# Pair-mask sums, test and subtraction on GpSimd in a graph network's first row stage

## Chip, cores and metric

The kernel runs on one core of one Trainium2 chip. The metric is device time in microseconds; the time given is the median of three runs.

## What is computed

The reference takes 1250 nodes of 512 features and 20,000 edges (`src`, `dst`). Four layers follow each other, each added to the rows: a message-passing layer over the edges, a layer of 64 routed experts, a graph network of four blocks, and a gated feed-forward layer with ternary weights. The change touches what the third layer needs from the edges. Its attention is sparse:

```
scores = einsum('ehd,ehd->eh', q[src], k[dst])
smax   = segment_max(scores, src);  ex = exp(scores - smax[src])
denom  = segment_sum(ex, src);      attn = ex / denom[src]
out    = segment_sum(attn[:, :, None] * v[dst], src)
```

The kernel computes it densely, over all 1250 x 1250 pairs of nodes. An edge that occurs c times counts c times, which is a term log(c) on the score; a pair without an edge must vanish, which is a very large term of the other sign. That term, for all pairs, is the mask. A node with no outgoing edge has an output of zero, for which a flag for each row (`linked`) is kept. All four blocks read the same mask.

## The kernel before

The rows are ten tiles of 125. While the earlier layers run, each edge is counted into one of two count tables in HBM (`pairs`, 1250 x 1250 float32 each). The first row stage (`rows_stage` with source "first" and sink "qkv") then does two things side by side.

**Its main work.** For each row tile VectorE and ScalarE make normalised and modulated rows, TensorE turns them, and ScalarE and VectorE write them as a high part and a low part (`y_high`, `y_low`; in a product of two such numbers three of the four part products are taken). VectorE's shift instruction is at L1873. Then TensorE works through 24 units (L1437), each three part products over four 128-row blocks: units 0 to 11 give q, units 12 to 23 give k, each in three spans of 500, 374 and 376 rows, with two PSUM banks in turn, so unit n waits until unit n-2 has been taken. ScalarE takes q units alone (`qT`, L1771); of k units ScalarE takes `k_high` (L1777) and VectorE then `k_low` (L1900). Before unit 12 wk must be split into high and low parts (`set_a_high` by ScalarE, `set_a_low` by VectorE, L1856, four pieces, placed after n = 7 in both engines' orders); before the v tiles wv is split likewise (`set_b`, placed after n = 21, behind the masks' work of that n). Wq's low parts come from GpSimd (L1624), which does nothing else here. The ten v tiles (L1446) end the stage: VectorE adds the bias (L1962), ScalarE copies the high part and VectorE subtracts the low one (L1973).

**The mask.** For tile t the two counts are loaded into `pair_c[t]` and `pair_m[t]`. VectorE adds them in place and keeps the row maximum in `pair_top` (L1908), ScalarE takes Ln(count + 1e-18) in place (L1784) and writes Relu(-1e28 log - 1e28) to `pair_m[t]` (L1786), which is zero where a pair has an edge, and VectorE subtracts the logarithm (L1914). SP stores the result in `mask_d`. Where this work stands in each engine's order is written by hand: after unit n of its loop, VectorE does the sums with COUNT_AT[t] = n and then the subtractions with CAP_AT[t] = n, ScalarE the logarithms with LOG_AT[t] = n. Each engine runs its instructions strictly in that order.

**Buffers and SP's order.** Twelve buffers serve ten tiles in pairs, so tiles 6 to 9 reuse buffers of tiles whose masks are stored. SP issues every load and store, in this order: loads of tiles 0 to 5, a store of the rows, stores of masks 0 to 3, load 6 (once mask 0 is stored), store 4, load 7 (once mask 1 is stored), the next conditioning weights `cw`, the v bias and wv, a wait until `cw` has landed, store 5, load 8 (once mask 2 is stored), load 9 (once masks 3 and 5 are stored), then stores 6 to 9. ScalarE's k_high of unit 12 waits until three masks are made, its copies of v tiles 0, 2, 4 and 7 until seven, eight, nine and ten are. The attention that follows (L2041, L2144, L2185) reads the masks from HBM; L2185 is GpSimd's scaling of the probabilities with 1/denominator and `linked`.

The semaphores `counted`, `logd`, `capped` and `mask_made` count the tiles through the four steps.

Of the kernel before, what the change touches and what calls it, by code (L numbers as in the profile page):

```python
# [17 lines left out]
ACT = mybir.ActivationFunctionType  # L18
ALU = mybir.AluOpType
# [3 lines left out]
P = 125  # L23
NT = N // P
# [1431 lines left out]
class Map:  # L1456
# [4 lines left out]
    def __init__(self, nc, base):  # L1461
# [32 lines left out]
        self.tiny, self.far = at("tiny", 153536, [128, 1]), at("far", 153568, [128, 1])  # L1494
# [4 lines left out]
COUNT_AT = (3, 4, 5, 6, 8, 9, 12, 13, 15, 17)  # L1499
LOG_AT = (4, 5, 6, 7, 9, 10, 13, 14, 16, 18)  # L1500
CAP_AT = (5, 6, 8, 9, 10, 11, 14, 16, 18, 19)
TINY, BIG = 1.0e-18, 1.0e28


def rows_stage(nc, T, M, source, sink, g_d, x_d, loads, late, bias, bqk, bvo, last=False, pairs=None, mask_d=None):
# [11 lines left out]
             "pair_in0 pair_in1 pair_in2 pair_in3 pair_in4 pair_in5 pair_in6 pair_in7 pair_in8 pair_in9 counted consts logd capped mask_made "  # L1517
             "mask_out0 mask_out1 mask_out2 mask_out3 mask_out4 mask_out5 mask_out6 mask_out7 mask_out8 mask_out9")
    with Stage(nc, names) as (cw_ready, cw_next, b_in, a_in, w_in, v_in, a_high, a_cut, b_high, b_cut, v_high, v_cut,
# [5 lines left out]
                              counted, consts, logd, capped, mask_made, mask_out0, mask_out1, mask_out2, mask_out3, mask_out4,  # L1525
# [19 lines left out]
        with nc.Block() as block:  # L1545
# [59 lines left out]
            def _(pool):  # L1605
# [36 lines left out]
                if masks:  # L1642
                    nc.gpsimd.memset(M.tiny[:], TINY).then_inc(consts, 1)
                    nc.gpsimd.memset(M.far[:], -BIG).then_inc(consts, 1)
# [81 lines left out]
            def _(act):  # L1726
# [53 lines left out]
                def logarithm(t):  # L1780
                    if t == 0:
                        act.wait_ge(consts, 2)
                    act.wait_ge(counted, t + 1)
                    s.activation(M.pair_c[t][:], M.pair_c[t][:], ACT.Ln, bias=M.tiny[0:P, :]).then_inc(logd, 1)  # L1784
                    act.wait_ge(logd, t + 1)
                    s.activation(M.pair_m[t][:], M.pair_c[t][:], ACT.Relu, bias=M.far[0:P, :], scale=-BIG).then_inc(capped, 1)  # L1786
# [62 lines left out]
            def _(dve):  # L1849
# [53 lines left out]
                def masking(n):  # L1903
                    for t in range(NT) if masks else ():
                        if n == COUNT_AT[t]:
                            c = M.pair_c[t][:]
                            dve.wait_ge(pair_in[t], 64)
                            v.tensor_tensor_reduce(c, c, M.pair_m[t][:], 1.0, 0.0, ALU.add, ALU.max,  # L1908
                                                   M.pair_top[:, t:t + 1]).then_inc(counted, 1)
                    for t in range(NT) if masks else ():  # L1910
                        if n == CAP_AT[t]:
                            c = M.pair_c[t][:]
# [747 lines left out]
```

## Time and profile before

| | before |
|---|---|
| median of 3 runs | 2878.57 us (2877.28 to 2882.2) |
| profiled execution | 2881.81 us, span of its trace 2880.0 us |
| mean granted TensorE clock | 0.945 of full |
| first row stage | 943 to 1096 us of the span |

A span is the time from the first to the last instruction of one profiled execution. Busy time of an engine leaves out its waits; a wait is the idle time just before an instruction, put down to what released it. PE is TensorE, PEld its weight loads, DVE is VectorE, ACT ScalarE, POOL GpSimd, SP SyncE, and `ps` is PSUM. A granted clock of 1.00 is TensorE at 2.4 GHz, 0.50 at 1.2 GHz.

### The profile page before, as it was taken

Reading aid. Unit: us, or ns where it says so; the run is one execution under the profiler, and the core shown is the slowest. Engines: PE = TensorE matmul, PEld = TensorE weight load, DVE = VectorE, ACT = ScalarE, POOL = GpSimd, SP = SyncE. Lnnn points to the kernel's source line nnn. Section 1 sums busy time; section 2 is a strip of 40 time slices with the busy share of each in tenths; the row PEclk is TensorE's granted clock in tenths of the full one; section 3 lists DMA queues with packets and bytes.
Section 4 is the critical chain, followed back from the end, with each engine's and each line's share of the span. In section 5 each row is a group of like instructions: output and inputs, shape, how many; then the busy total and the mean of one; then the engine's idle time right before and its main releaser. Section 6 shows DMA issues by size and latency. Waiting matters only on the chain. (4 is left out here: it accounts for less than half of the span.)

```text
span 2880.0 us, 38762 instructions
## 1 busy us (share of the span) xinstructions
PE 2520.4 (88%) x13585; PEld 2166.2 (75%) x13585; DVE 1861.9 (65%) x3526; ACT 1396.8 (49%) x2764; POOL 1139.5 (40%) x850
## 2 busy tenths in 40 slices
PE   3999999746766668999999999989999989998999
PEld 3788878546556557887877877978978878877997
DVE  2899999564651745767646777457776367667862
ACT  1566566422245635655436655346654356544431
POOL 2788888853673002226003243013260022363420
PEclk9999999867878789999999999999999999999999
DMA  7444344238535752102221011111022030121101
GB/s 253 89 86 86 74 91 83 20 92 268 128 91 175 196 157 62 45 1 72 68 61 46 18 55 53 52 53 36 18 71 68 20 89 19 45 82 34 56 13 35
DMA packets 172076, 220.33 MB, mean 77 GB/s; under 512 B 111791, under 2 KB 120426, under 8 KB 164465
## 3 DMA queue, kind: packets, MB, share of 16 engines
q1 hardware_dynamic: 85134, 189.35, 22.6%
q0 software_dynamic: 86752, 28.51, 5.8%
q8 instruction: 111, 1.82, 0.3%
q14 instruction: 79, 0.65, 0.1%
HBM read 177.10 MB, written 40.15 MB: 75 GB/s over the span
## 5 line engine op out<-in xcount | busy, mean ns | idle before, releaser
L2185 POOL TENSOR_SCALAR prob<-prob,rden,linked 125x1250 f32<-125x1250 f32 x160 | 223.5, 1397 | 955.6 <-DVE rden L2152 955.6
L579 POOL DMA_INDIRECT pairs<-late_cnt,late_idx x160 | 351.1, 2195 | 125.5 <-DMA pairs<-late_cnt,late_idx 75.7
L2103 ACT CAST prob_high<-ps 125x375 fp32r<-125x375 f32 (+1 forms) x480 | 231.1, 503 | 267.1 <-PE ps L2065 261.8
L2144 DVE CUSTOM_DVE_ANT_0 prob<-ps,mask 125x1250 f32<-125x1250 f32 x160 | 233.0, 1456 | 130.1 <-PE ps L2041 109.1
L2157 DVE TENSOR_TENSOR prob_low<-ps,prob_high 125x375 fp32r<-125x375 f32 (+1 forms) x480 | 269.6, 585 | 46.6 <-ACT prob_high L2103 46.6
L338 POOL DMA_INDIRECT Hg<-h_rows,dsti x160 | 230.1, 1438 | 117.3 <-issue 94.0
L2054 PE MATMUL ps<-ident,prob 125*125 125x125 f32 x1600 | 252.3, 273 | 17.3 <-POOL prob L2185 10.7
L2054 PEld LDWEIGHTS ps<-ident,prob 125*125 125x125 f32 x1600 | 232.3, 187 | 29.7 <-POOL prob L2185 22.9
L538 PE MATMUL ps<-onehot,mhi 125*128 125x512 f32 (+1 forms) x960 | 245.7, 364 | 6.1 <-DVE onehot L426 5.9
L538 PE MATMUL ps<-onehot,mlo 125*128 125x512 f32 (+1 forms) x960 | 238.8, 357 | 0.0
L2095 ACT ACTIVATE prob<-prob,top 125x1250 f32<-125x1250 f32 x160 | 214.7, 1342 | 46.3 <-DVE top L2144 37.6
L2065 PE MATMUL ps<-prob_high,v_high 125*128 125x376 f32 (+1 forms) x480 | 211.1, 440 | 4.6 <-ACT qT L2107 3.0
L2041 PE MATMUL ps<-k_high,q_high 128*125 128x512 f32 (+1 forms) x480 | 173.9, 362 | 28.5 <-DVE q_low L2133 19.0
L538 PEld LDWEIGHTS ps<-onehot,mhi 125*128 125x128 f32 x960 | 158.4, 191 | 42.6 <-issue 13.4
L538 PEld LDWEIGHTS ps<-onehot,mlo 125*128 125x128 f32 x960 | 157.5, 191 | 28.2
L2041 PE MATMUL ps<-k_low,q_high 128*125 128x512 f32 (+1 forms) x480 | 172.5, 359 | 0.0
L2041 PE MATMUL ps<-k_high,q_low 128*125 128x512 f32 (+1 forms) x480 | 171.6, 358 | 0.0
L2065 PE MATMUL ps<-prob_low,v_high 125*128 125x376 f32 (+1 forms) x480 | 169.0, 352 | 0.0
L2065 PE MATMUL ps<-prob_high,v_low 125*128 125x376 f32 (+1 forms) x480 | 169.0, 352 | 0.0
L426 DVE TENSOR_SCALAR onehot<-iota_n,srcf 125x1250 fp32r<-125x1250 int16 x120 | 121.0, 1030 | 24.3 <-PEq L71 12.1
L2041 PEld LDWEIGHTS ps<-k_high,q_high 128*125 128x125 f32 x480 | 90.9, 189 | 50.3 <-DVE q_low L2133 20.7
L2330 POOL TENSOR_SCALAR neg<-raw,qsc 128x128 bf16<-128x128 f32 x132 | 78.6, 614 | 119.3 <-DVEq L2352 119.3
(442 smaller groups left out, 5952.4 us busy)
## 6 DMA issues: line engine op xcount, KB each, us to landing
mask<-mask_d SPq DMA_DIRECT2D x40, 546.9 KB
sg_wd<-L_ffn_Wd SPq DMA_DIRECT2D x32, 512.0 KB, 7.2
w_ring<-L_ffn_Wd SPq DMA_DIRECT2D x16, 1024.0 KB, 14.8
w_ring<-L_ffn_Wu SPq DMA_DIRECT2D x16, 1024.0 KB, 5.8
pairs<-zeros POOLq DMA_DIRECT2D x18, 625.0 KB, 25.2
keyrow<-keys_d SPq DMA_DIRECT2D x40, 244.1 KB
kept<-g_d SPq DMA_DIRECT2D x40, 224.0 KB
g_d<-kept SPq DMA_DIRECT2D x30, 224.0 KB
```

The lines of the kernel that those rows point to most:

```text
L338: nc.gpsimd.indirect_dma_start(Hg[:, g % 2, j, :, :].rearrange("p c f -> p (c f)"), None, h_rows[:, :], bass.IndirectOffsetOnAxis(dsti[:, ...
L426: v.tensor_scalar(onehot[:, j, :], T.iota_n[0:P, :], srcf[:, column(g, j):column(g, j) + 1], None, ALU.is_equal).then_inc(hot_ready, 1)
L538: ins = nc.tensor.matmul(agg_chunk(T, a, c), part[:, u, j, a * 128:(a + 1) * 128], onehot[:, j, n0:n0 + nn], start=first and k == 0 and c < 2,
L579: nc.gpsimd.indirect_dma_start(pairs[a][:, :], bass.IndirectOffsetOnAxis(T.E.late_idx[:, c:c + 1], 0), T.E.late_cnt[:, c:c + 1], None, com ...
L2041: ins = nc.tensor.matmul(S(u)[0:P, n0:n0 + nn], M.qr[x][:, b % 2, i * P:(i + 1) * P], M.k[y][:, h, n0:n0 + nn], start=n == 0, stop=n == 2)
L2054: ins = nc.tensor.transpose(T.ps[0:P, 3 + s % 4, i * P:(i + 1) * P], M.prob[:, (FIRST[b] + i) % RING, j * P:(j + 1) * P], T.ident[0:P, 0:P])
L2065: ins = nc.tensor.matmul(T.ps[:, 7, 0:w], M.v[x][:, j, h * DH:(h + 1) * DH], M.pt[y][:, s % 3, 0:w], start=j == 0 and n == 0, stop=j == NT ...
L2095: s.activation(M.prob[:, u % RING, :], M.prob[:, u % RING, :], ACT.Exp, bias=M.top[:, u % RING:u % RING + 1], scale=-1.0, accum_out=M.den[ ...
L2103: s.copy(M.pt[0][:, n % 3, 0:w], T.ps[0:P, 3 + n % 4, 0:w]).then_inc(high, 1)
L2144: v.tensor_tensor_reduce(M.prob[:, r, :], S(u)[0:P, 0:N], M.mask[:, it % MASKS, :], 1.0, 3.0e38, ALU.add, ALU.min, M.top[:, r:r + 1]).then ...
L2157: v.tensor_tensor(M.pt[1][:, n % 3, 0:w], T.ps[0:P, 3 + n % 4, 0:w], M.pt[0][:, n % 3, 0:w].bitcast(F32), ALU.subtract).then_inc(low, 1)
L2185: nc.gpsimd.tensor_scalar(M.prob[:, r, :], M.prob[:, r, :], M.rden[:, r:r + 1], T.linked[:, it:it + 1], ALU.mult, ALU.mult).then_inc(norme ...
```

## The change

GpSimd adds the two count tiles, tests the logarithm and subtracts it. The sums of tiles 0 to 5 stand first, right behind its weight splits, then the masks of tiles 0 to 5, then sums 6 and 7, masks 6 and 7, sums 8 and 9, masks 8 and 9. The test is one tensor_scalar: 1e30 where the logarithm is below -1, zero elsewhere. ScalarE's Relu goes, and its logarithm leaves the sum of each row in `pair_top` with an accumulator output. `linked` is now whether that sum is above (N - 0.5) log(1e-18), that of a row without edges. VectorE has none of the mask's work left but `linked`. ScalarE's logarithms stand elsewhere in its order. Loads, stores and the waits on `mask_made` and `mask_out` are unchanged.

```diff
-        self.tiny, self.far = at("tiny", 153536, [128, 1]), at("far", 153568, [128, 1])
+        self.tiny = at("tiny", 153536, [128, 1])
...
-COUNT_AT = (3, 4, 5, 6, 8, 9, 12, 13, 15, 17)
-LOG_AT = (4, 5, 6, 7, 9, 10, 13, 14, 16, 18)
-CAP_AT = (5, 6, 8, 9, 10, 11, 14, 16, 18, 19)
-TINY, BIG = 1.0e-18, 1.0e28
+LOG_AT = (4, 4, 5, 5, 6, 7, 14, 15, 20, 21)
+TINY, BIG = 1.0e-18, 1.0e30
+UNLINKED = (N - 0.5) * math.log(TINY)
...
                 if masks:
+                    def count(t):
+                        pool.wait_ge(pair_in[t], 64)
+                        nc.gpsimd.tensor_tensor(M.pair_c[t][:], M.pair_c[t][:], M.pair_m[t][:], ALU.add).then_inc(counted, 1)
+
+                    def mask(t):
+                        pool.wait_ge(logd, t + 1)
+                        nc.gpsimd.tensor_scalar(M.pair_m[t][:], M.pair_c[t][:], -1.0, BIG, ALU.is_lt, ALU.mult).then_inc(empty, 1)
+                        pool.wait_ge(empty, t + 1)
+                        nc.gpsimd.tensor_tensor(M.pair_c[t][:], M.pair_m[t][:], M.pair_c[t][:], ALU.subtract).then_inc(mask_made, 1)
                     nc.gpsimd.memset(M.tiny[:], TINY).then_inc(consts, 1)
-                    nc.gpsimd.memset(M.far[:], -BIG).then_inc(consts, 1)
+                    for t in range(6):
+                        count(t)
+                    for t in range(6):
+                        mask(t)
+                    count(6)
+                    count(7)
+                    mask(6)
+                    mask(7)
+                    count(8)
+                    count(9)
+                    mask(8)
+                    mask(9)
...
                     act.wait_ge(counted, t + 1)
-                    s.activation(M.pair_c[t][:], M.pair_c[t][:], ACT.Ln, bias=M.tiny[0:P, :]).then_inc(logd, 1)
-                    act.wait_ge(logd, t + 1)
-                    s.activation(M.pair_m[t][:], M.pair_c[t][:], ACT.Relu, bias=M.far[0:P, :], scale=-BIG).then_inc(capped, 1)
+                    s.activation(M.pair_c[t][:], M.pair_c[t][:], ACT.Ln, bias=M.tiny[0:P, :],
+                                 accum_out=M.pair_top[:, t:t + 1]).then_inc(logd, 1)
...
-                def masking(n):
-                    for t in range(NT) if masks else ():
-                        if n == COUNT_AT[t]:
-                            c = M.pair_c[t][:]
-                            dve.wait_ge(pair_in[t], 64)
-                            v.tensor_tensor_reduce(c, c, M.pair_m[t][:], 1.0, 0.0, ALU.add, ALU.max,
-                                                   M.pair_top[:, t:t + 1]).then_inc(counted, 1)
-                    for t in range(NT) if masks else ():
-                        if n == CAP_AT[t]:
-                            c = M.pair_c[t][:]
-                            dve.wait_ge(capped, t + 1)
-                            v.tensor_tensor(c, M.pair_m[t][:], c, ALU.subtract).then_inc(mask_made, 1)
...
                 if masks:
-                    v.tensor_scalar(T.linked[:], M.pair_top[:], 1.0, None, ALU.min).then_inc(spare, 1)
+                    dve.wait_ge(logd, NT)
+                    v.tensor_scalar(T.linked[:], M.pair_top[:], UNLINKED, None, ALU.is_gt).then_inc(spare, 1)
```

## Rows read from the trace of the kernel before

**Rows 1.** The page, part 1: engine, busy us, share of the span, instructions.
```profile
PE 2520.4 (88%) x13585; PEld 2166.2 (75%) x13585; DVE 1861.9 (65%) x3526; ACT 1396.8 (49%) x2764; POOL 1139.5 (40%) x850
```

**Rows 2.** Busy time by stretch; last columns: granted clock, DMA share, GB/s.
```profile
943.00:966.00 23.00, 11.31 (x33) 7.54 (x34) 20.40 (x46) 11.37 (x22) 5.16 (x6) 0.50 0.91 232
1008.40:1064.10 55.70, 34.12 (x144) 30.20 (x145) 23.68 (x30) 21.75 (x26) 0.00 (x0) 0.79 0.72 201
1064.10:1096.00 31.90, 28.00 (x122) 22.08 (x120) 13.93 (x23) 7.31 (x13) 0.00 (x0) 0.98 0.00 1
```

**Rows 3.** Waits in the first row stage: who for whom, total us, times, longest.
```profile
PE ps L1437 <- DVE k_low L1900: 21.5, 4, 14.0
...
DVE pair_h L1908 <- DMA pair_c<-pairs: 14.5, 1, 14.5
...
PE ps L1437 <- ACT qT L1771: 7.5, 4, 3.5
```

**Rows 4.** Timeline of TensorE: start us, us, line and operation.
```profile
1049.33 1.59 PE L1437 MATMUL ps<-y_high,set_a_high 128*128 128x374 f32 x4 [14.03 <-DVE k_low L1900]
1050.72 1.45 PE L1437 MATMUL ps<-y_low,set_a_high 128*128 128x374 f32 x4
...
1055.45 0.85 PE L1437 MATMUL ps<-y_high,set_a_high 128*128 128x376 f32 x4
...
1064.13 1.09 PE L1446 MATMUL ps<-set_b_high,y_high 128*125 128x512 f32 x4
```

**Rows 5.** Timeline of SP's queue, the stores of masks 3 and 5.
```profile
1009.20 0.30 SPq L141 DMA_DIRECT2D mask_d<-pair_d  x1
...
1035.68 0.32 SPq L141 DMA_DIRECT2D mask_d<-pair_g  x1
```

**Rows 6.** Waits of SP's queue, 925 to 1110 us.
```profile
SPq L141 <- DMA cw<-L_gnn_cond: 13.4, 1, 13.4
```

**Rows 7.** Timeline of ScalarE from q unit 4 to the first logarithm.
```profile
983.78 0.57 ACT L1771 ACTIVATE qT<-ps,bqk 128x374 f32<-128x374 f32 x1 [1.49 <-PE ps L1437]
984.75 1.28 ACT L1784 ACT_TABLE_LOAD   x1 [0.39 <-DVE pair_top L1908]
986.04 1.34 ACT L1784 ACTIVATE pair_a<-pair_a,tiny 125x1250 f32<-125x1250 f32 x1
```

**Rows 8.** Groups of ScalarE by shape, 943 to 1110 us: busy us, mean ns.
```profile
L2095 ACT ACTIVATION_READ_ACCUMULATOR prob<-prob,top 125x1 f32 x3 | 0.6, 186 | 0.0
```

**Rows 9.** Groups of GpSimd by shape, whole span: count, busy us, mean ns, idle before.
```profile
L2185 POOL TENSOR_SCALAR prob<-prob,rden,linked 125x1250 f32<-125x1250 f32 x160 | 223.5, 1397 | 955.6 <-DVE rden L2152 955.6
L2330 POOL TENSOR_SCALAR neg<-raw,qsc 128x128 bf16<-128x128 f32 x132 | 78.6, 614 | 119.3 <-DVEq L2352 119.3
L1620 POOL TENSOR_TENSOR kept<-kept,bvo 125x512 f32<-125x512 f32 x40 | 53.7, 1360 | 13.4 <-ACT y_row L1748 12.7
```

**Rows 10.** Single source lines: duration in ns, min/median/max, first and last start.
```profile
L1610 POOL TENSOR_TENSOR o_low<-qT,o_high x40: 1157/1170/2153, 1297.7 to 2541.4; 128x500 fp32r<-128x500 f32 x40
...
L1919 DVE TENSOR_TENSOR cwr<-cw,cwr x8: 1214/1699/2198, 944.8 to 2512.2; 32x1024 fp32r<-32x1024 f32 x8
...
L1856 DVE TENSOR_TENSOR set_a_low<-set_a_raw,set_a_high x48: 675/685/1653, 1001.2 to 2579.8; 128x512 fp32r<-128x512 f32 x48
...
L1873 DVE SCALAR_TENSOR_TENSOR shift<-mv,rstd x80: 158/160/1149, 947.9 to 2559.9; 125x1 f32<-125x1 f32 x80
```

**Rows 11.** Timeline of GpSimd, the end of its work in this stage.
```profile
962.67 0.11 POOL L1644 MEMSET far<- 128x1 f32 x1
```

**Rows 12.** Timeline of all engines in a later row stage.
```profile
1301.60 1.74 POOL L1632 TENSOR_TENSOR kept<-kept,bvo 125x512 f32<-125x512 f32 x1
...
1302.22 2.19 DVE L1919 TENSOR_TENSOR cwr<-cw,cwr 32x1024 fp32r<-32x1024 f32 x1
```

**Rows 13.** Timeline of VectorE, the sums of tiles 8 and 9.
```profile
1047.19 1.46 DVE L1908 CUSTOM_DVE_ANT_0 pair_h<-pair_h,pair_c 125x1250 f32<-125x1250 f32 x1 [14.51 <-DMA pair_c<-pairs]
...
1052.42 1.45 DVE L1908 CUSTOM_DVE_ANT_0 pair_g<-pair_g,pair_d 125x1250 f32<-125x1250 f32 x1
```

More of the change, by code:

```diff
@@ L1516, in rows_stage @@
              "unit_made taken h_high h_cut v_made v_row v_top v_low spare "
-             "pair_in0 pair_in1 pair_in2 pair_in3 pair_in4 pair_in5 pair_in6 pair_in7 pair_in8 pair_in9 counted consts logd capped mask_made "
+             "pair_in0 pair_in1 pair_in2 pair_in3 pair_in4 pair_in5 pair_in6 pair_in7 pair_in8 pair_in9 counted consts logd empty mask_made "
              "mask_out0 mask_out1 mask_out2 mask_out3 mask_out4 mask_out5 mask_out6 mask_out7 mask_out8 mask_out9")
@@ L1524, in rows_stage @@
                               pair_in0, pair_in1, pair_in2, pair_in3, pair_in4, pair_in5, pair_in6, pair_in7, pair_in8, pair_in9,
-                              counted, consts, logd, capped, mask_made, mask_out0, mask_out1, mask_out2, mask_out3, mask_out4,
+                              counted, consts, logd, empty, mask_made, mask_out0, mask_out1, mask_out2, mask_out3, mask_out4,
                               mask_out5, mask_out6, mask_out7, mask_out8, mask_out9):
@@ L1781, in logarithm @@
                     if t == 0:
-                        act.wait_ge(consts, 2)
+                        act.wait_ge(consts, 1)
                     act.wait_ge(counted, t + 1)
-                    s.activation(M.pair_c[t][:], M.pair_c[t][:], ACT.Ln, bias=M.tiny[0:P, :]).then_inc(logd, 1)
-                    act.wait_ge(logd, t + 1)
-                    s.activation(M.pair_m[t][:], M.pair_c[t][:], ACT.Relu, bias=M.far[0:P, :], scale=-BIG).then_inc(capped, 1)
+                    s.activation(M.pair_c[t][:], M.pair_c[t][:], ACT.Ln, bias=M.tiny[0:P, :],
+                                 accum_out=M.pair_top[:, t:t + 1]).then_inc(logd, 1)
                 def logarithms(n):
@@ L1937, in _ @@
                 low(NT - 2)
-                masking(3)
                 finish(4)
@@ L1941, in _ @@
                 low(NT - 1)
-                masking(4)
-                masking(5)
                 for n in range(6, len(order)):
                     finish(n)
-                    masking(n)
                     if n == 7 and three:
```

## The prediction

> **What bounds the kernel now.** I read the page first, for the busy shares. TensorE is busy for 2520 of 2880 us [rows 1], so most stages are TensorE's own and only a stretch in which it stands idle can give time back. The diff touches one stage, the first row stage, 943 to 1096 us. The table of busy time by stretch [rows 2] cuts it where its work changes. From 943 to 966 the normalised rows are made. Up to 1008 TensorE works through the twelve q units, up to 1064 through the twelve k units (34.1 us of work in 55.7 us), and then through the ten v tiles (28.0 of 31.9 us, nearly solid). The reader should see that k is the loose stretch. The list of waits of this stage says why [rows 3]: TensorE waited 21.5 us for VectorE's k_low (14.0 us in one piece), and VectorE, ahead of that k_low in its own order, waited 14.5 us for the load of pair tile 8. A further 7.5 us went to ScalarE's late qT in the q units. So a summation of a tile that has not yet arrived stands in VectorE's queue in front of work that TensorE needs.
>
> The second thing to see is what ends the stage. The v tiles start at 1064.13 [rows 4], and in code order they need ScalarE's split of wv, which follows the logarithm of tile 9 whatever engine makes the counts. Tile 9 is loaded only after SP has seen the new conditioning weights land: it issued the store of mask 3 at 1009.20 and that of mask 5 only at 1035.68 [rows 5], having stood 13.4 us on the weights [rows 6]. Everything from mask 3 to that landing is loads and stores back to back, so the arrival of tile 8 follows the time of mask 3.
>
> **The change, part by part.** *Removed from VectorE*: ten sums with maximum of 1.45 us and ten subtractions of the same shape, 29 us in all, and with them the waits for late tiles in its queue. *Removed from ScalarE*: ten Relu passes, as wide as the logarithm of 1.34 us, against ten accumulator reads of 0.19 us [rows 7, 8], about 11.5 us. Both are cover in front of TensorE's k units, and by themselves would let the k units run nearly dense: up to 21.5 + 7.5 = 29 us of TensorE's idle time [rows 3]. I book none of it directly, because v does not wait for the k units but for log 9. The idle time moves behind them.
>
> *Added to GpSimd*: for each of ten tiles a sum, a test and a subtraction, 125x1250. It has no two-input row of that width. Its 125x512 add takes 1.36 us as a mean with stalls in it [rows 9]; the same ratio gives at most 3.3 us, the 1.16 us that a 128x500 one takes undisturbed [rows 10] gives 2.9, and a fixed part would take off a little more (2.75). I take 3.0 us. The test (less than, times) has two near rows, both GpSimd tensor_scalar. The one with two multiplications takes 1.40 us at 1250 wide, the one with a comparison takes 0.60 us at 128 wide [rows 9], which would be 5.9 us if all of it were per element, and about 2.8 us if the 0.3 us that a short instruction could cost were fixed. Bounds 1.4 and 5.9 us. The operand shape is that of the first, the operator that of the second; I take 2.0 us.
>
> The Trainium skill bears on the test (GPSIMD Engine Reference, section 7, "Performance pitfalls for Q7 kernels"): a loop body that produces compare results costs 2.03 cycles an element as against 1.03 when it is not unrolled. No row here isolates that. At that skill page's 1.2 GHz it would make the test an estimated 2.1 us plus its fixed part, and the sum below about +6 us in place of +3.6. The same page of the Trainium skill (section 3.1) has a 2048-wide add at 4497 ns, an estimated 2.75 us here, within the bounds above.
>
> *The start of the masks.* GpSimd's sums of tiles 0 to 5 begin at 962.8, behind its four splits and a memset [rows 11]. Weights and six tiles are 8.5 MB; at the 232 GB/s of the first stretch [rows 2] they are in by about 981, so sum 5 ends near 984. ScalarE ends unit 4 at 984.35, loads the table (1.28 us) and has log 0 and its read done at 987.2 [rows 7, 8]. The sums are thus hidden, and masks go from 987.2 at 2.0 + 3.0 + 0.1 = 5.1 us each. Mask 3 is made at 1007.6.
>
> *The collision.* VectorE and GpSimd get in each other's way when the VectorE instruction has two SBUF inputs. At 1302.22 VectorE's cwr subtraction took 2.19 us instead of 1.21, starting while GpSimd's kept add ran, and ending 1.1 us after that add ended; the add itself had taken 1.74 [rows 12, 10]. Set_a_low goes from 0.68 to 1.65 us in the same place, and even the one-column shift instruction reaches 1.15 us against 0.16 [rows 10]. The reader is to see strict turns: each waits for the other's current instruction. In this stage the two-input instructions of VectorE are the shifts, the eight splits (four of wk, four of wv) and v_low. GpSimd now has 3 us instructions in a row, so each split can wait up to 3 us. The wk splits, ready from ScalarE from 997 on, then end near 1008, and TensorE, which could have used them at about 1002, starts the k units at 1008 as before. They take 0.6 us from GpSimd on the way to mask 3 (the rest falls into waits): 1008.2, 1.0 us earlier than the 1009.2 of before [rows 5]. All of the chain through SP follows: **-1.0 us**.
>
> *The tail.* Tile 8 lands at 1046.2 (1047.2 before [rows 13]). Sum 8 to 1049.2. Tile 9 was there without a wait by 1052.4 [rows 13]; two loads of 0.6 MB each at the rate above put it 4 to 5 us behind tile 8, so 1050.5. Sum 9 to 1053.5, log 9 to 1055.1, first wv half split by ScalarE at 1055.7. But GpSimd is in mask 8: test to 1055.5, subtraction to 1058.6. VectorE's first wv split goes in there, to 1059.1; then the test of mask 9 to 1061.1, the second split 1061.7, the subtraction 1064.7, the third and fourth 1065.9. The v tiles start at 1066.0 instead of 1064.1: **+1.9 us**. Before, with no GpSimd work, 16.9 us lay between tile 8 and v, now 19.8.
>
> *The clock.* TensorE stands idle before v for some ten us. After such a pause the first groups of four 374-wide products took 1.59 and 1.45 us, the third as long as the second, against 0.85 of a warm one [rows 4], some 2 us lost; the table of stretches shows a granted clock of 0.79 over the k units, a mean of the 1.2 and 2.4 GHz levels [rows 2]. Before, v started warm. **+1.7 us**.
>
> The v tiles cover the rest: mask 9 is made at 1064.7, needed by ScalarE at the eighth v tile (about 1086). The unit 23 that waits for log 8 ends by 1055 and is covered by the same pause. If mask 9's cover were gone it would add its lateness. The one new wait on VectorE, for log 10 before the flags, has v_row queued behind it, but its wv splits end later than the log, so it costs nothing.
>
> Sum: -1.0 + 1.9 + 1.7 = +2.6, and 1 us for shift instructions held by GpSimd's sums at 965 to 977, where TensorE's next tile has 1.5 us of slack each (0 to 2): **+3.6 us**. The profiled execution took 2881.81 us (span 2880.0), so 2885.4 for one like it; on the median of the runs, 2878.57, it is 2882.2.
>
> **Rivals.**
> *Faster: the wv splits get through.* Place: VectorE's four splits before v. If the engines do not take strict turns there, or GpSimd is between instructions, v starts at 1055.1 + 2.1 + 0.7 = 1057.9, 6.2 us early, less 1.7 of clock: -4.5. With a test of 1.4 us mask 3 and all behind it are 2.4 us earlier still: -7, 2871.6. It passes -5.8 with a test below 1.7 us. For it: the waits taken from VectorE are real, and v stands 16.9 us behind tile 8 now. Against: the turns in [rows 12].
> *Slower: a dear test.* Each 0.1 us of the test costs 0.4 at mask 3 and 0.2 in the tail. From 2.4 us on, the sum passes +5.8; at 2.8 it is +8.4 (2887), at 3.5 +12.6 (2891), at 5.9 +27. For it: 0.60 us for 128 columns. Against: VectorE runs two-input work between these short ones, so they hold little.
> *Slower: the front slips.* If the held shifts cost TensorE more than their slack, log 0 and all masks slip with it: 3 us make +5.6 to +7, 2885.
>
> **How the numbers follow.** A measurement of this kernel tells 0.2% (5.8 us) from no change. Forecast (test between 1.4 and 2.3 us, sum 0 to +5.4): 0.50. Dear test 0.27, front 0.06, faster 0.17. So faster 0.17, same 0.50, slower 0.33. The range leaves out a tenth below, where only the full faster rival lies, and a tenth above, tests over 3.6 us: 2873 to 2892.
>
> **What would show it.** Right: no wait of VectorE for pair loads and of TensorE for k_low in one long piece; TensorE idle instead before unit 23 and before v, for 8 to 12 us; set_a_low and set_b_low with means over 1.5 us; GpSimd sums of 2.9 to 3.1 us; masks a little over 5 us apart; store of mask 3 at 1007 to 1010; first v product at 1064 to 1068 at half clock. Wrong, if the test is not 1.4 to 2.4 us, if set_b_low stays at 0.68, or if tile 8's arrival moves otherwise than mask 3.

## The result and the profile after

The change made the kernel slower: 2901.89 us median (2898.96 to 2906.63, 4 runs) against 2880.39 us, a ratio of 1.0074 with a 95% interval of 1.0059 to 1.009. The profiled execution took 2898.96 us, its span 2897.2 us, 17.2 us over that of before. A ratio is the median time of a kernel over that of the kernel before, the two timed side by side. Timed again beside later runs, the same kernel stood at 1.0049 (1.0035 to 1.0062). The forecast, 2882.2 us in a range of 2873 to 2892, is too low either way.

The page after, part 1. It answers to [rows 1]: GpSimd has 102 us more, ScalarE 12 us less, and VectorE no less although it has 30 instructions fewer, because others of its instructions are stretched (below).

```profile
PE 2518.6 (87%) x13585; PEld 2163.3 (75%) x13585; DVE 1865.2 (64%) x3496; ACT 1384.8 (48%) x2764; POOL 1241.8 (43%) x879
```

Busy time by stretch, cut where [rows 2] was cut by work: the k units, then the v tiles. Columns are PE, PEld, DVE, ACT, POOL, then granted clock, DMA share and GB/s.

```profile
1012.00:1079.40 67.40, 32.94 (x144) 29.65 (x144) 17.28 (x16) 14.54 (x24) 63.10 (x19) 0.73 0.57 162
1079.40:1113.00 33.60, 30.14 (x120) 23.70 (x120) 15.98 (x23) 6.29 (x11) 2.87 (x2) 0.93 0.06 19
```

The stretch of the k units grew from 55.7 to 67.4 us around the same work of TensorE, and GpSimd is busy for 63.1 of it: one engine now works almost without a gap where it had nothing. The timeline of GpSimd says with what.

```profile
963.51 2.84 POOL L1644 TENSOR_TENSOR pair_a<-pair_a,pair_l 125x1250 f32<-125x1250 f32 x1
...
992.07 4.48 POOL L1648 TENSOR_SCALAR pair_l<-pair_a 125x1250 f32<-125x1250 f32 x1 [8.07 <-ACT pair_a L1803]
996.63 2.88 POOL L1650 TENSOR_TENSOR pair_a<-pair_l,pair_a 125x1250 f32<-125x1250 f32 x1
999.60 4.44 POOL L1648 TENSOR_SCALAR pair_m<-pair_b 125x1250 f32<-125x1250 f32 x1
```

A sum takes 2.84 us and a subtraction 2.88, but the test 4.44. A mask is made every 7.5 us. ScalarE's first logarithm comes late as well, and SP's stores of masks 3 and 5 (in [rows 5] at 1009.20 and 1035.68) follow:

```profile
989.25 1.28 ACT L1803 ACT_TABLE_LOAD   x1
```
```profile
1022.65 0.30 SPq L141 DMA_DIRECT2D mask_d<-pair_d  x1
...
1048.99 0.32 SPq L141 DMA_DIRECT2D mask_d<-pair_g  x1
```

TensorE in the k units and at the first v product (in [rows 4] at 1064.13, without a wait and at full clock):

```profile
1012.17 1.95 PE L1437 MATMUL ps<-y_high,set_a_high 128*128 128x500 f32 x4 [4.67 <-DVE set_a_low L1874]
1043.19 1.59 PE L1437 MATMUL ps<-y_high,set_a_high 128*128 128x374 f32 x4 [16.26 <-DVE k_low L1918]
1065.75 1.59 PE L1437 MATMUL ps<-y_high,set_a_high 128*128 128x376 f32 x4 [8.48 <-DVE k_low L1918]
1079.40 2.07 PE L1446 MATMUL ps<-set_b_high,y_high 128*125 128x512 f32 x4 [9.56 <-DVE set_b_low L1874]
```

The long waits for k_low did not go away. The first (16.26 us) now ends with ScalarE's logarithm ahead of k_high, which waits for GpSimd's sum of tile 6 (17.41 us, below), and that sum stands in GpSimd's queue behind masks 0 to 5. The second (8.48 us, before unit 23) ends with the logarithm of tile 8, whose sum waited 2.10 us for its load. VectorE's two-input instructions, which [rows 10] has at 0.16 us (shift) and 0.68 us each (set_a_low), are held:

```profile
966.35 2.84 DVE L1891 SCALAR_TENSOR_TENSOR shift<-mv,rstd 125x1 f32<-125x1 f32 x1
972.00 2.87 DVE L1891 SCALAR_TENSOR_TENSOR shift<-mv,rstd 125x1 f32<-125x1 f32 x1
977.67 1.54 DVE L1891 SCALAR_TENSOR_TENSOR shift<-mv,rstd 125x1 f32<-125x1 f32 x1
981.23 2.79 DVE L1891 SCALAR_TENSOR_TENSOR shift<-mv,rstd 125x1 f32<-125x1 f32 x1
...
1000.98 11.14 DVE L1874 TENSOR_TENSOR set_a_low<-set_a_raw,set_a_high 128x512 fp32r<-128x512 f32 x4 [6.05 <-ACT set_a_high L1752]
...
1068.84 10.51 DVE L1874 TENSOR_TENSOR set_b_low<-set_b_raw,set_b_high 128x512 fp32r<-128x512 f32 x4 [3.24 <-ACT set_b_high L1752]
...
1080.31 2.08 DVE L1957 TENSOR_SCALAR linked<-pair_top 125x10 f32<-125x10 f32 x1
```
```profile
1040.28 1.34 ACT L1803 ACTIVATE pair_j<-pair_j,tiny 125x1250 f32<-125x1250 f32 x1 [17.41 <-POOL pair_j L1644]
```

**The stage in three pieces.** All kernels below are read the same way, from five start times of each trace: the stage's first conditioning product, ScalarE's table load before the first logarithm, SP's stores of masks 3 and 4, the first v product. Four of them bound the three pieces of the table; the store of mask 3 is used further below. Those of before and after:

```profile
946.12 1.22 PE L1678 MATMUL ps<-cwr,condT 81*125 81x512 f32 x2 [35.30 <-DVE cwr L1919]
```
```profile
946.93 1.22 PE L1697 MATMUL ps<-cwr,condT 81*125 81x512 f32 x2 [36.20 <-DVE cwr L1924]
```
```profile
1012.46 0.66 SPq L141 DMA_DIRECT2D mask_d<-pair_e  x1
```
```profile
1030.08 0.30 SPq L141 DMA_DIRECT2D mask_d<-pair_e  x1
```

| us | to the table load ("front") | table load to store 4 ("masks") | store 4 to v ("rest") | sum | ratio (95%) |
|---|---|---|---|---|---|
| before | 38.63 | 27.71 | 51.67 | 118.01 | 1 |
| after | 42.32 | 40.83 | 49.32 | 132.47 | 1.0074 (1.0059 to 1.009) |
| d1_after_again | 38.58 | 40.85 | 50.06 | 129.49 | 1.0049 (1.0035 to 1.0062) |
| a6_test_without_scaling | 38.39 | 35.33 | 49.45 | 123.17 | 1.0038 (1.0024 to 1.0052) |
| a1_mult_for_test | 41.44 | 25.41 | 50.25 | 117.10 | 0.9998 (0.9988 to 1.0009) |
| a2_relu_on_scalare | 39.29 | 19.44 | 49.98 | 108.71 | 0.9975 (0.9964 to 0.9986) |
| b1_sums_alone | 41.45 | 23.36 | 53.04 | 117.85 | 0.9998 (0.9988 to 1.0007) |
| a3_shift_one_tensor | 37.62 | 40.81 | 50.54 | 128.97 | 1.0034 (1.0021 to 1.0047) |
| c1_before_shift | 36.68 | 27.71 | 52.11 | 116.50 | 0.9976 (0.9965 to 0.9987) |
| a4_masks_89_after_splits | 38.37 | 40.84 | 42.67 | 121.88 | 1.0016 (1.0007 to 1.0025) |
| d2_shift_and_hold | 36.75 | 40.83 | 41.90 | 119.48 | 0.999 (0.9978 to 1.0003) |
| c3_before_cw_wait_late | 38.39 | 27.72 | 51.27 | 117.38 | 1.001 (1.0001 to 1.0019) |
| c4_after_cw_wait_late | 38.38 | 40.84 | 50.58 | 129.80 | 1.0048 (1.0034 to 1.0063) |
| a5_relu_shift_hold | 36.31 | 19.46 | 47.33 | 103.10 | 0.9935 (0.9922 to 0.9948) |
| c2_a5_cw_wait_late | 36.84 | 19.48 | 48.33 | 104.65 | 0.9918 (0.9903 to 0.9932) |

The piece "masks" repeats to 0.04 us in every kernel whose GpSimd does the same work there. It is the piece in which the time went: against before, the three pieces together have 14.5 us more in the first profile and 11.5 in d1, and this one alone 13.1 in both. The pieces come from one profiled execution each, the ratios from all runs.

### The profile page after: what moved, and what is told of

Its sections match the earlier page's. It is cut to its first block and busy times, and to the rows that moved or that the text cites. A ratio compares the mean times of both kernels' runs of the same rounds, so it can differ in the third digit from the quotient of the medians.

```text
span 2897.2 us, 38761 instructions
## 1 busy us (share of the span) xinstructions
PE 2518.6 (87%) x13585; PEld 2163.3 (75%) x13585; DVE 1865.2 (64%) x3496; ACT 1384.8 (48%) x2764; POOL 1241.8 (43%) x879
## 5 line engine op out<-in xcount | busy, mean ns | idle before, releaser
L2056 PE MATMUL ps<-ident,prob 125*125 125x125 f32 x1600 | 252.3, 273 | 17.2 <-POOL prob L2187 10.6
```

The source lines that it names most:

```text
L2056: ins = nc.tensor.transpose(T.ps[0:P, 3 + s % 4, i * P:(i + 1) * P], M.prob[:, (FIRST[b] + i) % RING, j * P:(j + 1) * P], T.ident[0:P, 0:P])
```

## The experiments

**m1_op_prices**: a small kernel of its own, not this one. GpSimd runs each form of the disputed instructions at 128, 512 and 1,250 columns by itself, then eight sums and eight tests beside instructions of VectorE.

> A small kernel of its own: it copies x to the output and otherwise only times instructions. GpSimd runs eight forms at 128, 512 and 1250 columns, VectorE idle; then GpSimd runs eight 1250-wide adds, and later eight tests, one behind the other, beside VectorE instructions of one and of two SBUF inputs. Theory dear comparison (the test costs 4.45 us for its comparison, per element): is_lt, mult takes 4.4 us at 1250 and 0.55 to 0.65 at 128; mult, mult with the same constants 1.3 to 1.5 us at 1250; min, mult like mult, mult. Rival dear constants (not the operator but immediate operands or something in place make it slow): mult, mult with constants is near 4.4 too, and 1.4 only with pointers. For the turns: the two-input subtraction of 0.68 us and the one-column two-input product take up to 2.9 us longer beside the adds, reciprocal and bn_stats nothing; the one-column product in the tensor_scalar form with a pointer is not held if only tensor inputs count.

Groups by shape, GpSimd: busy us, mean ns. L43 is less-than and times with constants, L44 times and times with constants, L45 the same with pointer scalars (the form of [rows 9]'s 1.40 us), L46 minimum and times, L47 less-than alone, L48 less-than with a pointer into bf16 (near [rows 9]'s 0.60 us), L49 the sum.

```profile
L43 POOL TENSOR_SCALAR c<-a 125x1250 f32<-125x1250 f32 x2 | 8.9, 4437 | 0.2
L46 POOL TENSOR_SCALAR c<-a 125x1250 f32<-125x1250 f32 x2 | 8.9, 4432 | 0.2
L48 POOL TENSOR_SCALAR h<-a,s 125x1250 bf16<-125x1250 f32 x2 | 6.9, 3442 | 0.2
L47 POOL TENSOR_SCALAR c<-a 125x1250 f32<-125x1250 f32 x2 | 6.7, 3367 | 0.2
L49 POOL TENSOR_TENSOR c<-a,b 125x1250 f32<-125x1250 f32 x2 | 5.6, 2816 | 0.2
L45 POOL TENSOR_SCALAR c<-a,s 125x1250 f32<-125x1250 f32 x2 | 2.8, 1391 | 0.2
L44 POOL TENSOR_SCALAR c<-a 125x1250 f32<-125x1250 f32 x2 | 2.5, 1240 | 0.2
L43 POOL TENSOR_SCALAR c<-a 125x128 f32<-125x128 f32 x2 | 1.3, 642 | 0.2
L48 POOL TENSOR_SCALAR h<-a,s 125x128 bf16<-125x128 f32 x2 | 1.2, 597 | 0.2
```

The same engine, the same operand shapes, and a factor of 3.6 between operators. From 128 to 1,250 columns the test grows by (4437 - 642) / 1122 = 3.38 ns a column, less-than alone by 2.52, two multiplications by 0.84. The comparison as such is not the cause, since the minimum costs as much, where the theory of the dear comparison had it as cheap as two multiplications. The fixed parts are 0.2 to 0.3 us (642 ns less 128 x 3.38 leaves 0.21). Of the 0.60 us row at 128 columns, L48 has 0.27 fixed and 0.33 per column, so the 0.3 us that the prediction supposed was about right. VectorE, beside GpSimd's sums (L78 to L82) and tests (L89):

```profile
L89 DVE TENSOR_TENSOR f<-d,e 125x512 f32<-125x512 f32 x4 | 9.8, 2447 | 13.7 <-POOLq L63 13.6
L80 DVE SCALAR_TENSOR_TENSOR f<-d,e 125x1 f32<-125x1 f32 x2 | 4.8, 2404 | 0.1
L82 DVE BATCH_NORM_STATS2 f<-d 125x6 f32<-125x512 f32 x2 | 1.4, 694 | 0.1
L79 DVE TENSOR_SCALAR f<-d,e 125x1 f32<-125x1 f32 x2 | 0.4, 214 | 0.1
```

A one-column instruction with two tensors in SBUF takes 2.40 us there; the same product with one of them as a pointer scalar takes 0.21. A one-input tensor_scalar of GpSimd holds VectorE as well as a two-input sum does. The means hide a pattern: one by one, the four subtractions beside the tests took 0.69, 4.20, 0.69 and 4.20 us. One that starts just ahead of a test is not held (and that test takes 4.87 us for 4.44); the next one ends with the test.

**a1_mult_for_test** and **a6_test_without_scaling**: only the length of the test changes. In both the mask that comes out is another one (a1 multiplies where the test compares, a6 leaves the factor out).

```diff
 # a1
-nc.gpsimd.tensor_scalar(..., -1.0, BIG, ALU.is_lt, ALU.mult)
+nc.gpsimd.tensor_scalar(..., -1.0, BIG, ALU.mult, ALU.mult)
 # a6
+nc.gpsimd.tensor_scalar(..., -1.0, None, ALU.is_lt)
```

> The changed kernel with the test's is_lt replaced by mult (the mask comes out wrong, the work is otherwise the same). Theory dear comparison: the test falls from 4.45 to 1.3 to 1.5 us, each of four masks before the store of mask 3 by 3 us and the two of the tail by 3 each: 18 to 20 us faster than the changed kernel, so 0.998 to 1.001 of the kernel before. Rival collisions (what costs is that GpSimd is busy beside VectorE at all, whatever the instruction): the splits stay as slow, set_a_low and set_b_low together 21.6 us, and the time falls by less than 8 us. Rival dear constants: the test stays at 4.4 and nothing changes.

> The kernel after with the test's second operation left out: is_lt alone, so the mask is wrong (0 or 1 where 0 or 1e30 belong). Measured by itself that form takes 3.37 us for 1,250 columns, between the 4.44 of the test and the 1.57 of the multiplication (1.0074 and 0.9998). Theory (the time follows the length of the test): 1.0074 less 0.0076 x (4.45 - 3.37)/(4.45 - 1.57) = 1.0045, within 0.001. Rival (a step: a load that is caught or missed, a split that is met by the tests or not): within 0.0008 of 1.0074 or of 0.9998.

The test took 1.24 us in a1 where nothing met it (1.57 us, the figure in the expectation of a6, is one that a split of VectorE stretched), 3.37 in a6 and 4.44 in the kernel after. The five tests in the piece from the table load to store 4 sum to 6.87, 17.34 and 22.58 us, the piece took 25.41, 35.33 and 40.83 us: 9.9 us for 10.5 and 5.5 for 5.2, one for one. The ratios went 0.9998, 1.0038, 1.0074 (or 1.0049, measured again). The pieces show a slope and no step; the ratios agree with it but do not settle its upper half, since a6 and 1.0049 overlap. With a cheap test the whole change costs nothing, and gains nothing. The rival of collisions fails as well: the four splits still took 9.61 and 8.26 us in a1, and yet the time came back in full, where that rival allowed less than 8 us.

**d1_after_again**: the kernel after once more, to see whether its late front belongs to it.

> The kernel after, unchanged, profiled and timed again. Theory A (which shifts are held depends on how GpSimd's sums fall between the landings of the pair tiles, and varies between executions): first logarithm 38 to 39 or 42 to 43 us after the stage's first condition matmul, v_proj 90 to 91.5 us after the logarithm's table load as before, ratio within 1.005 to 1.0075. Theory B (fixed by the kernel): 42.3 again, and 1.0074.

The front took 38.58 us, as long as before's, with one shift held in full and one in part (2.84, 0.16, 0.83, 0.16 us) where the first profile has four. What differs is a few hundredths of a us. GpSimd's six sums begin alike, but in the first profile sum 3 followed sum 2 at once, and the shift was ready at 972.00, 0.04 us behind its start:

```profile
969.13 2.86 POOL L1644 TENSOR_TENSOR pair_c<-pair_c,pair_k 125x1250 f32<-125x1250 f32 x1
971.96 2.88 POOL L1644 TENSOR_TENSOR pair_d<-pair_d,pair_j 125x1250 f32<-125x1250 f32 x1
```

In c4_after_cw_wait_late, whose front is the same code, that sum waited 0.32 us for its tile, the shift at 968.59 took 0.16 us, and the table load stood 38.38 us into the stage. In a4_masks_89_after_splits there was no gap, but its shift was ready at 969.89, 0.01 us ahead of sum 3, took 0.16 us, and the front is 38.37 us. a1 and b1, with neither, have 41.44 and 41.45. So one kernel can have either front, 3.7 us apart. The masks repeat to 0.02 us and the rest to 0.7. That is theory A, but for the ratio, which is just under its range.

**a3_shift_one_tensor** and **c1_before_shift**: one line of VectorE, in all eight row stages, put into the kernel after and into before.

```diff
-v.scalar_tensor_tensor(T.shift[:, t:t + 1], T.mv[:, t, 0:1], -1.0, T.rstd[:, t:t + 1], ALU.mult, ALU.mult)
+v.tensor_scalar(T.shift[:, t:t + 1], T.mv[:, t, 0:1], T.rstd[:, t:t + 1], -1.0, ALU.mult, ALU.mult)
```

> The kernel after with one line changed: the shift of a row tile is made by a tensor_scalar that takes 1/std as a pointer scalar instead of a second tensor operand (same value). Theory A (GpSimd's sums hold VectorE's one-column shift for up to 2.9 us, and that is how the front of the stage slips by about 4 us): the shifts of tiles 5 to 8 take about 0.2 us instead of 2.84, 2.87, 1.54 and 2.79; the first logarithm's table load comes 3 to 4 us earlier in the stage; the ratio to before falls from 1.0074 by 0.0006 to 0.0015, no more, because GpSimd's own queue of sums and tests still ends at the same place relative to its loads. Theory B (GpSimd's queue alone sets the rest, the front is cover): shifts short, table load earlier, but the ratio stays within 0.0004 of 1.0074.

> The kernel before with the shift of a3_shift_one_tensor, in all eight row stages. In a3_shift_one_tensor that line was worth more than booked (1.0074 to 1.0034, 11.5 us, of which 3.5 to 4 in the first row stage), and the line's busy time in the seven later stages fell from 24.1 to 15.0 us. Theory (GpSimd's own work holds the one-column shift there too, on VectorE's row chain): before, which holds it for 23.2 us in those stages and 3.8 in the first, gains 4 to 8 us: ratio 0.997 to 0.9985. Rival (the later stages cover it, and a3's surplus was scatter between executions): 0.9995 to 1.0005.

Every shift takes 0.21 us, and the front shrinks to 37.62 and 36.68 us. The ratio of a3 fell by more than either theory gave, 1.0074 to 1.0034; from the 1.0049 of d1 it is 0.0015, the most that theory A allowed. c1 shows where more can come from: the line is held in the later stages too, beside GpSimd work that before already had. From the attention's first table load to the end of the span before took 1783.4 us, after 1783.1, d1 1784.3; with the new line a3 took 1775.5, c1 1776.1, a5 1774.6 and d2 1776.1. (Of the other profiles without it, a2 at 1769.2 and c4 at 1778.6 lie low as well, so one profile alone would not show it; c1's interval does.) In c1 the line's 80 instructions take 17.1 us, all of one length:

```profile
L1873 DVE TENSOR_SCALAR shift<-mv,rstd 125x1 f32<-125x1 f32 x80 | 17.1, 214 | 2.9
```

**a2_relu_on_scalare** and **b1_sums_alone**: parts of the change. a2 gives the test back to ScalarE as the Relu it was and leaves sums and subtractions on GpSimd; b1 leaves only the sums there.

```diff
 # a2
-nc.gpsimd.tensor_scalar(M.pair_m[t][:], M.pair_c[t][:], -1.0, BIG, ALU.is_lt, ALU.mult)   # in mask(t)
+s.activation(M.pair_m[t][:], M.pair_c[t][:], ACT.Relu, bias=M.far[0:P, :], scale=-BIG)    # behind the logarithm
 # b1: as a2, and
-nc.gpsimd.tensor_tensor(M.pair_c[t][:], M.pair_m[t][:], M.pair_c[t][:], ALU.subtract)
+v.tensor_tensor(c, M.pair_m[t][:], c, ALU.subtract)                                       # at CAP_AT = (6, 6, 8, ...), before: (5, 6, 8, ...)
```

b1 also has LOG_AT as before, where a2 has that of the kernel after; both have BIG at 1e28 again.

> The changed kernel with the test put back on ScalarE (the Relu pass of before behind each logarithm); GpSimd sums and subtracts only. Theory (GpSimd's time per tile sets the chain through mask 3, the loads and the tail): a mask costs GpSimd 2.9 us in place of 7.4, ScalarE 1.34 more. Mask 3 stored near 1001 to 1003, tile 8 in near 1040, v from 1055: 0.996 to 0.998 of the kernel before (6 to 10 us faster). Rival (ScalarE's extra pass in front of the units takes back what GpSimd gains, since the logarithms stand in ScalarE's order before the takes): 1.000 to 1.003.

> The sums alone go to GpSimd; the Relu stays on ScalarE and the subtraction on VectorE at the units where before had them; the flags are read from the logarithm's row sums. Theory (the sums cost 2.8 us each and hold VectorE's shifts, but nothing of GpSimd's stands beside the splits): set_a_low and set_b_low take 2.5 us for four as before; the front slips by 3 to 4 us; VectorE is free of ten reductions; ratio 0.996 to 0.999. Rival (the subtractions were the part worth moving): ratio 1.000 to 1.002, above a2_relu_on_scalare's 0.9975 by more than 0.002.

a2 is faster than before, 0.9975. ScalarE has the test done in 1.34 us, and GpSimd's subtraction follows each logarithm in time: masks in 19.44 us in place of 27.71. b1 is level with before, 0.9998: the sums on GpSimd by themselves bring nothing. In b1 the masks are 4.35 us earlier than in before, the front is 2.8 us later, from held shifts, and store 4 to v takes 1.4 us more. So b1's rival holds in what it says (the subtractions were the part worth moving), though its ratio lies between the two numbers on record. The order of the logarithms differs between a2 and b1 too, and no run tells the two apart.

**a4_masks_89_after_splits** and **d2_shift_and_hold**: GpSimd waits for the wv splits before it touches masks 8 and 9; d2 has the shift of a3 too.

```diff
+pool.wait_ge(v_cut, KD)
 mask(8)
 mask(9)
```

> The changed kernel with one wait more: GpSimd starts masks 8 and 9 only when VectorE's four wv splits are done. Theory turns (the splits lose 8 us to GpSimd's four instructions there): set_b_low takes 2.5 us in place of 10.5, the v tiles start 8 us after the logarithm's split in place of 11, and the kernel is 7 to 11 us faster than the changed one: 1.003 to 1.005 of the kernel before. Rival (mask 9 then comes too late: made near 1087, needed by ScalarE's copy of v tile 7): the gain is given back and it stays at 1.007.

> The kernel after with the one-tensor shift (a3) and masks 8 and 9 held until the wv split is done (a4), the test still on GpSimd. Theory (the parts add: front as in a3, 37.6 us to the table load; table load to v_proj 83.5 us as in a4, of which the test's length is what is left over before's 79.4): ratio 0.9985 to 1.000, since the shift gives about 0.9976 of before by itself and a4 alone was 1.0016. Rival (holding the masks gives nothing once the front is earlier, because the transfers then set the end): 1.002 to 1.0035, as a3 alone.

TensorE's wait for set_b_low fell from 9.56 us to 1.66 in a4 and 1.56 in d2. a4's ratio, 1.0016, is below the 1.003 to 1.005 expected. The piece from store 4 to v gives 7 to 8 us, and a4 has the short front besides; from d1's 1.0049 it is a fall of 0.0033, 9.5 us, inside the 7 to 11 us expected. The timeline of d2, VectorE and TensorE:

```profile
1066.69 2.50 DVE L1875 TENSOR_TENSOR set_b_low<-set_b_raw,set_b_high 128x512 fp32r<-128x512 f32 x4 [3.26 <-ACT set_b_high L1753]
```
```profile
1069.24 2.07 PE L1446 MATMUL ps<-set_b_high,y_high 128*125 128x512 f32 x4 [1.56 <-DVE set_b_low L1875]
```

Store 4 to v takes 42.67 and 41.90 us in place of 50. The v products still begin at half clock, so the pause is shorter but not gone. Masks 8 and 9 now hold VectorE's first two v_low instead (3.76 and 3.08 us in d2 against 0.68), behind the start of v. The parts add: d2 has the front of a3 and the rest of a4, and its ratio is level with before (0.999). Not all of that is the stage won back, for the shift gains in the later stages too: against c1, which has the same shift, d2 stands at 0.999 / 0.9976 = 1.0014, and its three pieces are 119.48 us against 116.50.

**c3_before_cw_wait_late** and **c4_after_cw_wait_late**: SP's wait for the conditioning weights, which stands ahead of the store of mask 5 and of the loads of tiles 8 and 9 ([rows 6]: 13.4 us), goes behind the last store.

```diff
-sp.wait_ge(cw_next, 48)              # at the end of late()
+sp.wait_ge(cw_next, 48)              # behind the waits for mask_out
```

> The same move of SyncE's wait alone, in the kernel before. TensorE waited 14.03 us for k_low there behind the logarithm of tile 8 (14.85 us for its sum). Theory: store 5 leaves at about 1024 instead of 1035.68, the loads of tiles 8 and 9 with it, v_proj starts 8 to 12 us earlier: ratio 0.996 to 0.9975. Rival (the transfers are what is slow): 0.999 to 1.0005.

> The same move in the kernel after, where mask 5 is subtracted at about 1034 to 1037, 12 to 15 us ahead of its store at 1048.99. Theory (SyncE's queue carries GpSimd's lateness of mask 4 through the wait for the condition weights to tiles 8 and 9): v_proj 6 to 11 us earlier, ratio 1.0035 to 1.0055 against 1.0074. Rival (GpSimd's own queue of tests is by then what is last, since sums 8 and 9 stand behind masks 6 and 7): 1.0065 to 1.0075.

Store 5 left at 1021.83 in c3 (before: 1035.68), the load of pair_c at 1029.46 (before: 1038.29), and the sum of tile 8 still began at 1045.94, 100.4 us into the stage against 101.1:

```profile
1021.83 0.43 SPq L141 DMA_DIRECT2D mask_d<-pair_g  x1
...
1029.46 0.34 SPq L141 DMA_DIRECT2D pair_c<-pairs  x1
```
```profile
1045.94 1.46 DVE L1909 CUSTOM_DVE_ANT_0 pair_h<-pair_h,pair_c 125x1250 f32<-125x1250 f32 x1 [14.88 <-DMA pair_c<-pairs]
```

The theory is wrong in c3, whose ratio is 1.001 (1.0001 to 1.0019), a little above the rival's range: SP's wait stood where tile 8 would have waited anyway. But the rival's "slow transfers" are not a full set of DMA engines. The stretches just before store 5 in before and before tile 8 landed in c3 (columns as above, the last two DMA share and GB/s):

```profile
1031.00:1035.50 4.50, 4.30 (x20) 3.93 (x18) 0.74 (x1) 1.49 (x3) 0.00 (x0) 0.77 0.06 25
```
```profile
1036.00:1043.00 7.00, 0.00 (x0) 0.00 (x0) 0.00 (x0) 0.00 (x0) 0.00 (x0) 0.70 0.06 27
```

The share is 0.06, what one of the sixteen DMA engines would give, where it is 0.98 over 1037 to 1045 in before. In before the packets of that stretch are almost all of 4,096 bytes, a row of the conditioning weights, one behind the other; in c3 they are, by their sizes, the last of the v bias, of wv and of tile 8. So, as an inference (no view names the single DMA engine), the three loads of `cw` (68 KB each, an estimated 8 us at 25 GB/s) go through one of them, which falls behind, and every later load with a part on it ends late. No run spreads them. c4's 1.0048 had looked like the theory's, but its pieces are those of after with the short front, and d1 without any edit measured 1.0049; it shows no gain either.

**a5_relu_shift_hold** and **c2_a5_cw_wait_late**: the better version. a5 is a2 with the shift of a3 and the hold of a4; c2 has c4's move as well.

> Three edits of the kernel after together: the test back on ScalarE as a Relu (alone 0.9975), the shift as in a3_shift_one_tensor, and GpSimd's subtractions of masks 8 and 9 held until the wv split is done. If what GpSimd still costs is the hold on VectorE, the parts add up: 0.9975 less 0.001 for the front and less 0.0012 for set_b_low (4.7 us for its four in a2_relu_on_scalare, 2.5 before): about 0.995 to 0.9965. If ScalarE is the bound there (its Relus and casts ahead of qT, for which TensorE waited 3.46, 4.03 and 1.52 us), the ratio stays at 0.997 to 0.998 and only the named waits change their releaser.

> a5_relu_shift_hold with SyncE's wait for the condition weights' three transfers moved behind the last mask store, so that mask 5's store and the loads of tiles 8 and 9 no longer stand behind it. Theory (TensorE's 7.92 us wait for k_low is that wait: loads 8 and 9 late, the logarithm of tile 8 late on ScalarE): store 5 about 12 us earlier, the wait gone, v_proj 6 to 9 us earlier, ratio 0.990 to 0.992 against 0.9935. Rival (the transfers share the same engines, so that wv or tiles 8 and 9 land no earlier): 0.9925 to 0.994.

a5 is at 0.9935 (2860.93 us) and c2 at 0.9918 (2858.74 us). Both beat before and after. a5 is below the 0.995 to 0.9965 expected, which booked the shift for the first stage alone. Of its gain c1's shift is 0.0024, which the kernel before could have without any work moved; what is left of it for GpSimd's share is 0.9935 / 0.9976 = 0.996. c2's ratio lies where its theory put it (0.990 to 0.992), but its interval and a5's overlap, and by the pieces (47.33 and 48.33 us from store 4 to v) the move of the wait gave nothing. In c2 TensorE still waits 8.95 us before the unit behind the logarithm of tile 8, and that logarithm is still late by its load.

## Why the prediction was wrong

**The failed step: the price of the test.** It was taken at 2.0 us between rows of 1.40 us (two multiplications, 1,250 wide) and 0.60 us (a comparison, 128 wide), "the operand shape is that of the first, the operator that of the second". It measured 4.44 us. On GpSimd the operator sets the price per column, so the row with the comparison was the one to scale: 2.54 ns a column and 0.27 us fixed in L48, 3.44 us for this width, and 1.07 us more for the second operation (4437 less 3367 ns, L43 and L47). The prediction had that row and that fixed part, but its "about 2.8 us" was too little even by them (0.3 + 0.30 / 128 x 1250 is 3.2), it left out that the test has a second operation, and it then took a middle value nearer to the row of the other operator.

The Trainium skill (GPSIMD Engine Reference, section 7) puts loop bodies that produce compare results at 2.03 cycles an element, and at 1.03 when unrolled twice. At that page's 1.2 GHz the measured slopes are an estimated 1.0 cycle a column for two multiplications, 3.0 for less-than alone and 4.1 for the test, so the dear end is half as much again to twice the page's 2.03. The prediction's estimate from the page was 2.1 us plus a fixed part, the test 4.44; the measurement decides.

**What the prediction's own formula gives with 4.45 us.** The "dear test" rival, at 0.27, was the case that came, and at the masks its mechanism holds. It prices each 0.1 us at 0.4 us at mask 3 and 0.2 in the tail, so 24.5 such steps make 9.8 - 1.0 = +8.8 us at the store of mask 3. Table load to that store measured 24.45 us before and 33.40 after, +8.95. In the tail, from tile 8 to v, it would give 19.8 - 16.9 + 4.9 = +7.8 us. Store of mask 3 to v measured 54.93 us before, 56.75 after and 57.51 in d1: +1.8 to +2.6. The tail is overpriced. GpSimd there, and VectorE's four splits one by one:

```profile
1066.92 4.44 POOL L1648 TENSOR_SCALAR pair_c<-pair_h 125x1250 f32<-125x1250 f32 x1
1071.44 3.12 POOL L1650 TENSOR_TENSOR pair_h<-pair_c,pair_h 125x1250 f32<-125x1250 f32 x1
1074.65 4.77 POOL L1648 TENSOR_SCALAR pair_d<-pair_g 125x1250 f32<-125x1250 f32 x1
1079.50 2.86 POOL L1650 TENSOR_TENSOR pair_g<-pair_d,pair_g 125x1250 f32<-125x1250 f32 x1
```
```profile
1068.84 2.45 DVE L1874 TENSOR_TENSOR set_b_low<-set_b_raw,set_b_high 128x512 fp32r<-128x512 f32 x1 [3.24 <-ACT set_b_high L1752]
1071.21 0.68 DVE L1874 TENSOR_TENSOR set_b_low<-set_b_raw,set_b_high 128x512 fp32r<-128x512 f32 x1
1071.81 3.31 DVE L1874 TENSOR_TENSOR set_b_low<-set_b_raw,set_b_high 128x512 fp32r<-128x512 f32 x1
1075.04 4.31 DVE L1874 TENSOR_TENSOR set_b_low<-set_b_raw,set_b_high 128x512 fp32r<-128x512 f32 x1
```

The first split was ready at 1068.84, when test 8 was half through, and v started at the end of test 9 (1079.42), not of the subtraction behind it as the prediction had it. The four splits waited for less than three instructions of GpSimd: the second began between test 8 and the subtraction and took its free 0.68 us. With 4.44 us tests the prediction's strict turns would have put one split behind each of four instructions. The whole formula says +18.3 us against a span 17.2 us longer, and 15.5 in d1. That it comes so near is in part luck, as its terms show: masks +8.95 for 8.8, tail +1.8 for 7.8 (6.8 after the slip below), front +3.7 for 1, clock +2.2 for 1.7. A tail priced too high stands against a front priced too low.

**A slip in the sum.** v at 1066.0 was worked out from tile 8 at 1046.2, which is already 1.0 us early. The +1.9 us thus holds the -1.0 us, and the sum takes it off once more. By its own terms the prediction should have read +4.6 us, 2883.2, and the formula above +19.3. This is 1 us, against 14.7 for the test.

**The front.** Booked at 1 us for held shifts with 0 to 2 as its bounds; measured +3.7 us in one profile and 0 in another. The mechanism was right, the slack of 1.5 us a tile was not enough: four shifts in a row lost 9.4 us of VectorE's time, and TensorE then waited for y_row three times (0.88, 0.47 and 0.92 us) where it had not before.

**Right.** Sum and subtraction at 3.0 us (2.8 to 2.9, up to 3.2 where a split met one). Both splits are held: 11.14 and 10.51 us for four in place of 2.5, though not in strict turns. Loads and stores behind mask 3 pass its lateness on one for one: to the issue of the last load it is 33.85 us before and 33.67 after. That piece was put down to SP's 13.4 us wait; c3 shows that the wait did not set it, which makes no difference to the sum here. The clock: the first v products took 2.07, 1.91 and 1.54 us against 1.09, and v to the exponentials' table load 34.66 us against 32.48, +2.2 for 1.7 booked. The idle time of TensorE did move behind the k units. That no long wait for k_low would be left was wrong: GpSimd's sums 6 and 7 stand behind six masks, and ScalarE's logarithm behind them, a queue that the prediction did not follow since it watched v alone. It cost nothing here, since TensorE waited again before unit 23.

What stays open: why the same kernel measured 1.0074 in one set of runs and 1.0049 in another. The medians moved from 2901.89 to 2898.1 us after and from 2880.39 to 2883.99 before, so about half of the 0.0025 came from the kernel before. The 3.7 us of the front would make the other half, but only the profiled executions show a front.

## What to carry to other kernels

Price a GpSimd instruction from a row with the same operators, scaled by its columns, not from one of the same shape: here 1.24 us or 4.44 us for one 125x1250 tensor_scalar, by its first operation alone. Before work goes to GpSimd, list what VectorE runs beside it with two tensors in SBUF, however small, since each such instruction can wait for a whole GpSimd one; a pointer scalar in place of the second tensor took a one-column instruction from up to 2.87 us to 0.21, and was worth 0.24% in the kernel before, where it had been up to 1.15 us. When a sum is put together, ask of each term whether a time in it already holds another term. When a wait in a DMA queue precedes late data, move it once and look at the landing, not at the issue, and at the DMA share while the data are missing.

## What the runs showed of the hardware

GpSimd's minimum with a multiplication is as slow as the comparison (4432 and 4437 ns). A GpSimd instruction with one input holds VectorE like one with two: VectorE's 125x512 subtraction, 0.68 us where nothing holds it (v_low, before), took 2447 ns as a mean beside tests, as 0.69 and 4.20 us in turn. VectorE's tensor_scalar with constants on 125x10 was held for 2.08 us after and 3.60 us in d2 (0.16 before), while the one with a pointer scalar stayed at 0.21 beside the same engine. The two differ in width as well (10 columns and one), and no run tells which of the two matters. And a tile's load issued 8.8 us earlier (c3) landed 1.25 us earlier, 0.6 by the stage's own clock.
